# Attention of a gated block scaled and added in two VectorE passes, its first layer norm on ScalarE, its text norms summed ahead of the loop

## The reference

```python
v = ln(x) @ Wv.T + bv            # 128 features per token
t = ctx @ Wt.T + bt
cos = (v @ t^T) / max(|v| |t|, 1e-8)       # 256 x 256 per batch entry
x = x + tanh(g_xattn) * cos
x = x + tanh(g_ffn) * (shared(ln(x)) + routed(ln(x)))
```

## Time and profile before

| | us |
|---|---|
| median of 3 runs | 631.09 |
| the three runs | 624.83, 632.0, 631.09 |
| span of the profiled execution | 625.3 |
| first attention step on DVE | 45.39 |
| last attention step on DVE | 122.16 |
| sigmoid of the router's scores | 136.44 |

### The profile page before, as it was taken

The page is one execution under the profiler, slowest core; times in us unless marked ns, Lnnn a source line. Parts: engine busy times, 40 slices in busy tenths (PEclk is TensorE's granted clock), DMA queues, the critical chain, the costliest instruction groups (busy, mean ns, idle before and its releaser), DMA issues.

```text
span 625.3 us, 12373 instructions
## 1 busy us (share of the span) xinstructions
PE 565.5 (90%) x3334; PEld 360.7 (58%) x3335; DVE 383.4 (61%) x874; ACT 250.9 (40%) x546; POOL 302.8 (48%) x396
## 2 busy tenths in 40 slices
PE   4998899899999997578999999999999999889995
PEld 2566678664555554235666666666666555445553
DVE  2449999768888764325555555555555366545664
ACT  3455664762256552223433343333433332223331
POOL 1015473424277777755444444444440266652662
PEclk9798797899999999669999999999999999999999
DMA  8941242232027463023333333333452133271342
GB/s 223 296 172 35 109 158 103 101 121 84 34 87 236 119 184 100 4 70 104 109 105 105 101 108 103 108 101 109 102 105 69 44 79 107 76 238 31 111 144 68
DMA packets 52366, 69.72 MB, mean 112 GB/s; under 512 B 8256, under 2 KB 44416, under 8 KB 52336
## 3 DMA queue, kind: packets, MB, share of 16 engines
q1 hardware_dynamic: 42816, 48.41, 24.1%
q0 software_dynamic: 8944, 18.83, 11.9%
q10 hardware_dynamic: 576, 2.10, 0.9%
HBM read 46.30 MB, written 23.01 MB: 111 GB/s over the span
## 4 chain that ended last, share of the span: by engine, by line
PE 51%; DVE 16%; issue 14%; POOL 8%; DMA 4%; ACT 3%; another core or an unknown queue 1%; SPq 1%; POOLq 1%; DVEq 0%; ACTq 0%
PE bank L1393 14%; PE bank L1476 14%; PE bank L1414 8%; PE bank L1496 6%; POOL ROWS L546 4%; DMA WR<-in_ctx_t 2%; POOL X L454 2%; PE bank L1485 2%; PE bank L1465 2%; DVE WR L826 2%; PE bank L1251 1%; DVE st L854 1%; DMA ROWS<-yrow,ixc 1%; DVE G L1064 1%
## 5 line engine op out<-in xcount | busy, mean ns | idle before, releaser
L1393 PE MATMUL bank<-XTC,WS 128*128 128x512 f16 x768 | 180.4, 385 | 1.4 <-issue 1.4
L1414 PE MATMUL bank<-WS,GS 128*128 128x256 f16 x768 | 98.1, 280 | 28.2 <-DVE GS L1070 15.7
L1393 PEld LDWEIGHTS bank<-XTC,WS 128*128 128x128 f16 x768 | 76.1, 99 | 82.0 <-issue 7.5
L1476 PE MATMUL bank<-WR,XTB 128*128 x474 | 115.4, 379 | 6.3 <-DVE XTB L1130 3.8
L520 POOL DMA_INDIRECT ROWS<-xrow,ixb x79 | 77.1, 976 | 65.4 <-POOL ixb L517 59.9
L1414 PEld LDWEIGHTS bank<-WS,GS 128*128 128x128 f16 x768 | 74.0, 100 | 58.7 <-DVE GS L1070 25.8
L1064 DVE SCALAR_TENSOR_TENSOR G<-bank,SIL 128x512 f32<-128x512 f32 x63 | 43.5, 690 | 71.8 <-ACT SIL L681 57.6
L1137 DVE SCALAR_TENSOR_TENSOR G<-bank,SIL 128x256 f32<-128x256 f32 x79 | 33.6, 425 | 84.2 <-ACT SIL L736 47.0
L546 POOL DMA_INDIRECT ROWS<-yrow,ixc x64 | 64.0, 1001 | 37.9 <-issue 21.6
L681 ACT ACTIVATE SIL<-bank 128x512 f32<-128x512 f32 x63 | 37.6, 596 | 111.6 <-PE bank L1393 88.6
L496 POOL DMA_INDIRECT slot_token<-tks,ixs x64 | 70.3, 1098 | 23.5 <-issue 17.1
(11 more groups left out here) (146 smaller groups left out, 735.6 us busy)
## 6 DMA issues: line engine op xcount, KB each, us to landing
STAGE<-in_routed_w SPq DMA_DIRECT2D x48, 256.0 KB
yrow<-ROWS SPq DMA_DIRECT2D x79, 128.0 KB, 1.7
X<-in_x SPq DMA_DIRECT2D x4, 1024.0 KB, 13.9
xrow<-STAGE SPq DMA_DIRECT2D x8, 512.0 KB, 2.9
xtd<-STAGE SPq DMA_DIRECT2D x8, 512.0 KB, 2.6
out<-X SPq DMA_DIRECT2D x7, 512.0 KB
WR<-in_ctx_t SPq DMA_DIRECT2D x4, 768.0 KB, 12.3
WR<-in_shared_w SPq DMA_DIRECT2D x3, 1024.0 KB, 15.4
```

The source lines that it names most:

```text
L1393: last = pe.matmul(acc[:, :], WS[:, wx, at:at + P], XTC[:, u, xx, k, :], start=(k == 0 and m == 0), stop=(k == KD - 1 and m == 2))
L1414: last = pe.matmul(acc, GS[:, a, gx, i * P:(i + 1) * P], WS[:, wx, at:at + D], start=(j == 0 and m == 0 and i % 2 == 0), stop=(j == J - 1 ...
L1476: last = pe.matmul(bank[u][:, :], XTB[:, u, xx, k, :], w, start=(k == 0 and m == 0), stop=(k == KD - 1 and m == 2))
```

## The change

- The squares of the text are multiplied by a full matrix of ones, so that each chunk's squared norms arrive along the other axis and repeated over all partitions, 128x512 per chunk. ACT takes the root of each (`text_norm`), DVE floors it and takes its reciprocal (`inverse_text_norm`) into `RB`, 128x4096 in all. `diagonal`, `row_norms` and `scales` are gone.
- `attend` on DVE computes min(RB, cap) times the dot products into `M`, with cap = 1e8 |v| per token, and then X + M * rv: eight instructions of 128x256 instead of four. POOL's `add_attention` is gone, and POOL is left with `cut`.
- The first layer norm is an ACT instruction with scale and bias (`normalise`), with bias = -mean/deviation from a small DVE operation.
- DVE's loop takes `weights_lo` after the second statistics. After the loop, the last `weights_lo` stands behind the last `attend`, where it stood ahead of it.
- SBUF is laid out anew: the squares, XL and XT share room with the rows and blocks of later stages.

```diff
+        SQT = LATE[:, 0:2 * CW].rearrange("p (a b) -> p a b", a=2)
+        XL = LATE[:, 2 * CW:4 * CW].rearrange("p (a b) -> p a b", a=TPC)
+        XT = LATE[:, 4 * CW:6 * CW].rearrange("p (a b) -> p a b", a=KD)
         VT = arena([CW])
         SQV = arena([CW])
         M = arena([TPC, D])
-        DG = arena([TPC, P])
 
...
@@ -431,41 +433,14 @@
                                    base=2 - k, pattern=[[-4, NBLK // 4]], channel_multiplier=1).then_inc(c_mem, 1)
             pool.iota(rev[:, :], pattern=[[-1, E]], base=E, channel_multiplier=0,
                       allow_small_or_imprecise_dtypes=True).then_inc(c_ready, 1)
-            def diagonal(c, first=False):
-
-                if first:
-                    pool.wait_ge(rt_ready, 1)
-                else:
-                    pool.wait_ge(rb, c)
-                pool.tensor_tensor(DG, ident[:, :].unsqueeze(1).to_broadcast([P, TPC, P]),
-                                   rt[:, ds(c * TPC, TPC)].unsqueeze(2).to_broadcast([P, TPC, P]),
-                                   ALU.mult).then_inc(dg, 1)
-
...
-            def add_attention(c):
-                for u in range(2):
-                    pool.wait_ge(cos_done, c * 2 + (u + 1))
-                    xs = X[:, ds(c * TPC + 2 * u, 2), :]
-                    pool.tensor_tensor(xs, xs, M[:, 2 * u:2 * u + 2, :], ALU.add).then_inc(added, 1)
-
-            diagonal(0, True)
-            diagonal(1)
-            add_attention(0)
-            diagonal(2)
-            with pool.Fori(1, NC - 2) as c:
-                add_attention(c)
-                cut(c - 1)
-                diagonal(c + 2)
-            add_attention(NC - 2)
-            cut(NC - 3)
-            add_attention(NC - 1)
-            cut(NC - 2)
-            cut(NC - 1)
+            with pool.Fori(0, NC) as c:
+                cut(c)
...
@@ -568,6 +543,10 @@
                     act.wait_ge(t_norm, c - 1)
                 act.activation(SQT[:, u, :], bank[u][:, :], ACT.Square, bias=btc[:, :]).then_inc(t_sq, 1)
 
+            def text_norm(c):
+                act.wait_ge(t_norm, c + 1)
+                act.activation(RB[:, c * CW:(c + 1) * CW], T_NORMS[c % 2][:, :], ACT.Sqrt).then_inc(t_sqrt, 1)
+
             def deviation1(i):
                 tiles = slice(*NORM_TILES[i])
                 act.wait_ge(ve1_ready, i + 1)
@@ -596,16 +575,16 @@
                     act.wait_ge(rv_ready, c)
                 act.activation(vn[:, :], bank[2][:, 0:TPC], ACT.Sqrt).then_inc(vn_sq, 1)
 
-            def scales(c, first=False):
-                act.wait_ge(rv_ready, c + 1)
-                act.wait_ge(rb, c + 1)
-                for u in range(2):
-                    if not first:
-                        act.wait_ge(added, c * 2 + (u - 1))
-                    for i in range(2):
-                        last = act.activation(M[:, 2 * u + i, :], bank[6][:, u * D:(u + 1) * D], ACT.Copy,
-                                              scale=rv[:, 2 * u + i:2 * u + i + 1])
-                    last.then_inc(m_ready, 1)
+            def normalise(c, group=2):
+
+                act.wait_ge(ln1_ready, group)
+                if not (isinstance(c, int) and c == 0):
+                    act.wait_ge(t1, c * 2)
+                for k in range(TPC):
+                    t = c * TPC + k
+                    last = act.activation(XL[:, k, :], X[:, ds(t, 1), :].rearrange("p a n -> p (a n)"), ACT.Identity,
+                                          bias=shift1[:, ds(t, 1)], scale=rstd1[:, ds(t, 1)])
+                last.then_inc(xln, 1)
 
             def lag(c, first=False):
                 for u in range(2):
...
             lead_v(2)
             lead_norm(2)
             deviation(1)
             weights_hi(2)
-            with act.Fori(2, LAST) as c:
+
+            def step(c, ahead=True):
                 lead(c + 1)
-                scales(c)
                 lag(c - 1)
                 lead_v(c + 1)
+                if ahead:
+                    normalise(c + 2)
                 lead_norm(c + 1)
                 deviation(c)
                 weights_hi(c + 1)
-            scales(LAST)
+
+            with act.Fori(2, LAST - 1) as c:
+                step(c)
...
@@ -795,6 +788,13 @@
                 ins.then_inc(s1, 1)
                 dve.wait_ge(s1, own1[0])
 
+            def inverse_text_norm(c):
+                part = slice(c * CW, (c + 1) * CW)
+                dve.wait_ge(t_sqrt, c + 1)
+                dve.tensor_scalar(RB[:, part], RB[:, part], TINY, None, ALU.max).then_inc(t_floor, 1)
+                dve.wait_ge(t_floor, c + 1)
+                dve.reciprocal(RB[:, part], RB[:, part]).then_inc(rt_ready, 1)
+
             def statistics(g):
                 dve.wait_ge(ld_x[g], 16)
                 for t in range(g * (NT // 4), (g + 1) * (NT // 4)):
...
-
-            def normalise(c, first=False):
-                if not first:
-                    dve.wait_ge(t1, c * 2)
-                for k in range(TPC):
-                    t = c * TPC + k
-                    last = dve.tensor_scalar(XL[:, k, :], X[:, ds(t, 1), :].rearrange("p a n -> p (a n)"),
-                                             mean1[:, ds(t, 1)], rstd1[:, ds(t, 1)], ALU.subtract, ALU.mult)
-                last.then_inc(xln, 1)
-
-            def inverse_norm(c, first=False):
+                dve.scalar_tensor_tensor(out=shift1[:, tiles], in0=mean1[:, tiles], scalar=-1.0, in1=rstd1[:, tiles],
+                                         op0=ALU.mult, op1=ALU.mult).then_inc(ln1_ready, 1)
+
+            def inverse_norm(c):
+
                 dve.wait_ge(vn_sq, c + 1)
-                if not first:
-                    dve.wait_ge(m_ready, c * 2)
+                dve.tensor_scalar(cap[:, :], vn[:, :], TINY, INV_EPS, ALU.max, ALU.mult)
                 dve.tensor_scalar(vn[:, :], vn[:, :], TINY, None, ALU.max).then_inc(rv_own, 1)
                 dve.wait_ge(rv_own, c + 1)
                 dve.reciprocal(rv[:, :], vn[:, :]).then_inc(rv_ready, 1)
 
-            def attend(c):
+            def attend(c, first=False):
+                dve.wait_ge(rv_ready, c + 1)
+                dve.wait_ge(rt_ready, NC)
                 for u in range(2):
                     dve.wait_ge(dot, c * 2 + (u + 1))
-                    dve.wait_ge(m_ready, c * 2 + (u + 1))
-
+                    if not first:
+                        dve.wait_ge(added, c * 2 + (u - 1))
                     for i in range(2):
-                        last = dve.scalar_tensor_tensor(out=M[:, 2 * u + i, :], in0=M[:, 2 * u + i, :], scalar=INV_EPS,
+                        last = dve.scalar_tensor_tensor(out=M[:, 2 * u + i, :], in0=RB[:, ds(c * CW + u * D, D)],
+                                                        scalar=cap[:, 2 * u + i:2 * u + i + 1],
                                                         in1=bank[u][:, i * D:(i + 1) * D],
                                                         op0=ALU.min, op1=ALU.mult)
                     last.then_inc(cos_done, 1)
+                for u in range(2):
+                    dve.wait_ge(cos_done, c * 2 + (u + 1))
+                    for i in range(2):
+                        xs = X[:, ds(c * TPC + (2 * u + i), 1), :].rearrange("p a n -> p (a n)")
+                        last = dve.scalar_tensor_tensor(out=xs, in0=M[:, 2 * u + i, :],
+                                                        scalar=rv[:, 2 * u + i:2 * u + i + 1], in1=xs,
+                                                        op0=ALU.mult, op1=ALU.add)
+                    last.then_inc(added, 1)
 
             def statistics2(c):
                 for u in range(2):
...
@@ -884,42 +888,36 @@
 
             statistics(0)
             variances(0)
+            inverse_text_norm(0)
+            inverse_text_norm(1)
             statistics(1)
             dve.wait_ge(tanh_done, 1)
             dve.tensor_scalar(tbv[:, :], bvc[:, :], tg[:, 0:1], None, ALU.mult)
             dve.tensor_scalar(tgs[:, :], tg[:, 1:2], 1.0 / WSCALE, None, ALU.mult).then_inc(tgs_done, 1)
             inverse_deviations(0)
-            normalise(0, True)
             statistics(2)
+            inverse_text_norm(2)
+            inverse_text_norm(3)
             statistics(3)
             variances(1)
-            normalise(1)
             inverse_deviations(1)
-            dve.wait_ge(t_sqrt, 1)
-            link1(dve.tensor_scalar(tn[:, :], tn[:, :], TINY, None, ALU.max))
-            dve.reciprocal(rt[:, :], tn[:, :]).then_inc(rt_ready, 1)
-            inverse_norm(0, True)
-            attend(0)
-            normalise(2)
+            for c in range(4, NC):
+                inverse_text_norm(c)
+            inverse_norm(0)
+            attend(0, True)
             statistics2(0)
             inverse_norm(1)
             normalise2(0, True)
             weights_lo(0)
-            with dve.Fori(1, LAST - 1) as c:
+            with dve.Fori(1, LAST) as c:
                 attend(c)
-                normalise(c + 2)
+                statistics2(c)
```

(24 more changed lines are left out.)

46 lines of the change are left out of this document (26 added, 20 removed).

## The result

| | before | after |
|---|---|---|
| median (us) | 631.1 of 4 runs (624.8 to 632.0) | 642.9 of 4 runs (641.3 to 645.5) |
| ratio of after to before | | 1.022, 95% interval 1.015 to 1.029 |
| span of the profiled execution | 625.3 | 643.8 |
| first attention step on DVE | 45.4 | 58.9 |
| last attention step | 122.2 | 135.9 |

The interval lies above 1 and on both sides of 2%: after is slower, but whether by more than 2% is open. The medians of this table are 1.9% apart. The two profiled executions are 18.5 us apart and the medians 11.7: after was profiled in the slowest of its four runs, and before's span lies in the lower part of its own.

What follows compares the result with a forecast made beforehand. It took the work ahead of the router's sigmoid as deciding, with DVE pacing the loop. Start-up +15.5, loop -8, tail +6.5, plus 1 for dot products, gave +15 on the median 631.1: 646 us, range 631 to 662.

Steps and rivals of the forecast that it cites:

- Start-up: Up to DVE's first attention step: eight wide floors and reciprocals, 32 us partly hidden, make it 15.5 us later.
- tail: Last attention step to the router's sigmoid: PE waits for the moved last weights part and loses clock, +6.5 us.
- loop: Seven intervals between DVE's attention steps: 68.5 us against 76.8, two at 8.0 and five at 10.5, so -8 us.
- The slope of 6.7 ns a column: Start-up on DVE: narrow reciprocals' cost per column extended to 512 columns, giving about 3.5 us for each wide reciprocal.
- The further 1 us put down for the dot products of chunk 1: On PE: these run at half clock after PE has waited for the reciprocals, adding 1 us.
- The streaming rival: Start-up on DVE: a wide reciprocal streams at 0.7 us, so the total is 624 to 631 us; chance 0.12.
- the ring: Loop: chain of PE and ACT work with hand-overs, 9.3 us per interval at full clock, PE idle about 1.5 us.
- DVE's 8.0: Loop: DVE's own work per interval after the change, 8.0 us, expected to set the first two intervals.
- its extreme form: Loop: PE's clock falls in every interval, 13.3 us each, sum +28, 659 us; chance 0.20.
- The blocking by POOL: Loop: POOL's remainder holding up DVE's new additions, at most 2.2 us in an interval, taken as zero.
- One to one to the end: Behind the router's sigmoid: nothing there is edited, so the sigmoid's shift carries whole to the end.
- The rival that the delay is taken up later: Behind the sigmoid: a wait not hanging on it absorbs the delay, sum 0 to +8 us; chance 0.08.

Runs made afterwards that it cites:

- experiment 2: The changed kernel without its eight wide reciprocals, the floor kept, so the output differs; median 630.2 us, 0.999 of before.
- experiment 4: The changed kernel with ten idle matmuls of constants on PE in each loop round, where PE waits for ACT's layer norm; median 635.4 us, 1.012 of before.
- experiment 3: The changed kernel with ACT's layer norm of chunk c+2 moved to right behind lead of c+1; median 626.6 us, 0.995 of before.
- experiment 1: The changed kernel with the last weights_lo on DVE ahead of the last attention step, as before the change; median 638.5 us, 1.011 of before.
- experiment 7: The changed kernel with the edits of experiment 1, experiment 3 and experiment 6 together; median 619.6 us, 0.984 of before.
- experiment 6: The changed kernel with text norms the old way (narrow root and reciprocal, diagonals, ones matmul) and an ACT copy per chunk; median 631.9 us, 0.993 of before.
- experiment 8: The kernel before with POOL's attention addition replaced by four DVE instructions; median 633.1 us, 1.004 of before.

## Why the prediction was right, and where its terms were off

The time forecast was 646 us and the median is 642.9, inside the range. The line of 2% was put at 643.7 us: the median lies just under it, the ratio of 1.022 just over it, so "slower by about 2%" held and "by more than 2%" is open. Start-up and tail held. The loop was wrong in size, and that error was cancelled by how the profiled executions stand to the medians: that the total came so close is in part luck.

**Start-up: forecast +15.5, measured +13.6.** The slope of 6.7 ns a column, read from 8, 24 and 32 columns, gave 3.5 us for 512 and the trace has 3.35. The floor took 0.39 and not 0.5. From start to start the eight pairs take 29.5 us instead of 32. Against that, x arrived 0.9 us later than in the profile of before (13.17 instead of 12.30), which no part of the change explains; the other terms held to within 0.4 us in sum. The further 1 us put down for the dot products of chunk 1 was not paid: the first interval is 7.95 us. In a sentence of its own: eight cycles a column, read from the Trainium skill, "VectorE: DVE Perf Modes", section "First, the fixed hardware budget", gave an estimate of 4.3 us, and the trace goes against it. The streaming rival (0.7 us) falls with this row, and experiment 2 shows that these instructions are what the start costs.

**Loop: forecast -8, measured +0.2. This is the step that failed in its size.** The prediction put the ring at 9.3 us at full clock, the idle time at 1.5 us, and took 10.5 "as if it fell in nearly a third" of the intervals. (The terms of the ring, as written, add up to 9.2.) Measured: two intervals ran near DVE's 8.0, the first and the last and not the first two, 16.6 us together against 16.0; the other five took 60.4 against 52.5. Two things made that. First, ACT's normalising takes 2.07 us and not the 1.57 I had taken from the row of L606, whose instructions have the same shape but one operand per partition (`rv`) where the new ones have two (`shift`, `rstd`), and which read a bank where the new ones read SBUF. As groups, of before and of after:

```profile
L606 ACT ACTIVATE WR<-bank,rv 128x256 f32<-128x256 f32 x32 | 12.6, 484 | 0.9 <-PE bank L1284 0.9
```

```profile
L585 ACT ACTIVATE LATE<-X,shift,rstd 128x256 f32 x16 | 8.3, 593 | 0.0
```

That is 109 ns more for each instruction. Most of it is the operand: in before L588 with one and L591 with two, both 128x512 from the same bank, take 691 and 776 ns. The 0.5 us is on the ring, and brings it near the 9.6 us of experiment 4. The Trainium skill, "ScalarE: Activation LUTs", section "What ACT_TABLE_LOAD costs", gives about 93 ns for each such pointer operand; the trace agrees roughly. Second, the clock was low in each of the five inner intervals, not in a third: granted 0.64 in the first of them and 0.77 in the four with the 1.66 us, and each of these four is 3.0 us longer than the 9.6. Of the 7.9 us that the five exceed the forecast, some 1.5 are the longer ring and the rest is the clock. The mechanism was the one foreseen: PE idle ahead of the first transpose with ACT as releaser, then half clock. I gave its extreme form 0.20 and should have given it more. Beside the row that I used (1.50 us idle, then half clock) the trace of before has 1.47 us at 22.54 and 1.55 at 94.56, and at half clock the dot products behind the latter took 3.76 us: each idle time of about 1.5 us that I had was followed by half clock, and the one to come was bound to come back in each interval. The Trainium skill, "TensorE: Matmul & The Clock Gate", section "HAM oscillation — how this bites in real kernels", describes a loop that falls back in each round because of its wait. The trace agrees in that the four rounds with the same wait all fell back. But the wait on that page is 3 to 5 us, and the one here 1.66: the page doesn't cover so short a wait. The size of that rival was over-read: 12.6 us, not 13.3, and 9.9 in the first of the five.

That DVE alone would run at 8.0 us held: 7.95 in the first interval, and 8.2 in four of seven once the wait was gone (experiment 3). The blocking by POOL, put at zero, cost little: the operation on four columns that follows the aggregation (L867) took up to 0.89 us beside the remainder, where 0.17 is its own time, and DVE had idle time to pay for it.

**Tail: forecast +6.5, measured +7.2.** The first shared step came 6.4 us after the last attention step (forecast 6.3), PE idled 5.2 us (forecast about 5), and the row from there to the sigmoid took 15.1 us (forecast 14.5). Experiment 1 shows the cause.

**One to one to the end.** From the sigmoid to the end before takes 488.9 us, after 486.4, and the kernels of all experiments between 484 and 491. The rival that the delay is taken up later falls: the sigmoid moved over 28 us between the kernels, and what follows it over 7.

**The sum.** The terms give +21.0 at the sigmoid instead of +15. In the medians +11.7 is left. 2.5 us of this went behind the sigmoid. The rest is that after's profiled execution was the longest of its four and before's among its shorter. I had added the 6 us between before's span and its median to the forecast. Of these, 1.7 hold for every kernel, since each time lies 1.7 us above the span of its own execution (645.5 and 643.8 for after). The other 4 are right only if the changed kernel was profiled as low among its runs, and it was not; its runs keep within 4.2 us in all. So two errors, in the loop and in this step to the median, had opposite signs; the terms, not the total, are what to judge.

## What to carry to other kernels

Work taken off the busiest engine shortens a loop only as far as the next ring allows; write that ring down with its hand-overs, and ask whether its wait leaves PE idle in every round, for then it can be paid for at half clock. The cure is a place in a list: moving one call on ACT (experiment 3) gave 16 us in the median, moving one on DVE (experiment 1) 4, and the arithmetic that the change moved gave nothing without them, even with the wide reciprocals left out (0.999 in experiment 2). Price a wide divide by the slope of narrow ones, and an instruction by a row with the same number of per-partition operands, not only of the same shape.

## What the runs showed of the hardware

- A reciprocal on DVE does not stream: 193 ns for 8 columns, 353 for 32, 3353 for 512, which is 6.3 ns for each further column, where a two-input pass of 128x512 takes 692 ns.
- An idle time of PE under 2 us can be followed by half clock: 1.66 us was in four rounds of four in after (and at the same place in the rounds of experiments 1 and 2), 1.50 and 1.55 us were in before, and 0.94 us once in the start-up of experiment 7, with half clock until about 35 us. Constant matmuls in the hole kept the clock up. The length of one idle time doesn't decide it alone: 0.70 us (experiment 6) and 0.67 us (experiment 1) left the clock alone, and so did longer ones in the start-up of after:

```profile
16.32 1.98 PE L1248 MATMUL bank<-WR,wt 96*128 96x512 f32 x4 [2.21 <-DMA WR<-in_ctx_t]
23.44 1.98 PE L1248 MATMUL bank<-WR,wt 96*128 96x512 f32 x4 [1.70 <-DMA WR<-in_ctx_t]
```

- A matmul of 128x128 fp32 constants leaves two records of 0.12 us, a transposition of the same size one.
- DVE's `tensor_scalar` can stand still beside POOL: 3.19 us for 1.38 of work in experiment 8, one instruction of 0.40 taking 2.22 beside POOL's 2.12. The Trainium skill, "SBUF — State Buffer", section "Who interferes with whom", calls this an exclusive lock of a shared port pair; the trace agrees.
